# Two of four FFN block pairs issued one step sooner, with their tile's projections, in a hand-ordered recurrent and FFN kernel

## The reference, cut to what matters

```python
xn = layernorm(x)                                   # x: (2, 2048, 256)
s  = timemix(xn)                                    # RWKV-7 mixing, with a recurrence over time
g  = silu(ffn(xn))
return x + s * g

def timemix(x):
    dx  = x_last - x;  mix = tanh((x + dx*x_miu) @ x_A)
    miu = lambdas + einsum(mix, x_B)                # 6 mixes
    r_in, w_in, k_in, v_in, a_in, g_in = x + dx * miu
    v = v_in @ vW.T;  r = r_in @ rW.T;  g = tanh(g_in @ g_A) @ g_B
    w = -softplus(-(w_miu + tanh(w_in @ w_A) @ w_B)) - 0.5
    k = normalized(k_in @ kW.T + tanh(k_in @ k_A) @ k_B)
    a = sigmoid(a_time + a_in @ a_A @ a_B) * 2
    kk = k * exp(min(w*0.5, 0))
    # per head, S is 64x64:  S = S*exp(w) + (S@-k) (k*a)^T + v kk^T ;  y = S @ r
    y = wkv7(r, w, kk, v, -k, k*a)
    return (groupnorm(y) + bonus(r, k, v)) * g @ oW.T

def ffn(x):                                         # 8 experts, top 2, rank-16 corrections
    top2 = top_k(softmax(x @ gate_w.T + gate_b))
    for e in top2: out += gate_e * (relu(x@wi.T + bi + x@lora_A[e].T@lora_B[e].T) @ wo.T + bo)
```

## Time and profile before

| | |
|---|---|
| median of 3 runs | 1036.86 us (1034.81 to 1039.39) |
| the profiled execution | 1039.15 us |
| its span, first to last instruction | 1037.4 us |
| PE busy | 997.8 us, 96% |
| DVE busy | 839.3 us, 81% |
| ACT busy | 664.8 us, 64% |
| POOL busy | 457.1 us, 44% |
| granted TensorE clock, mean | 0.987 of full |
| chain that ended last, PE's share | 91% |

### The profile page before, as it was taken

One profiled execution on the slowest core, in us unless ns is written; L12 is line 12 of the kernel. 1 busy time (PEld: TensorE's weight loads), 2 busy tenths in 40 slices (PEclk: granted clock), 3 DMA queues, 4 the chain that ended last, 5 costly groups with the idle time before them and its releaser, 6 DMA issues.

```text
span 1037.4 us, 45407 instructions
## 1 busy us (share of the span) xinstructions
PE 997.8 (96%) x19910; PEld 781.1 (75%) x19910; DVE 839.3 (81%) x1674; ACT 664.8 (64%) x1461; POOL 457.1 (44%) x541
## 2 busy tenths in 40 slices
PE   5799999999999999999999999999999999999896
PEld 3487777778787787877777787777878778787674
DVE  4377888888888797988888898888889879798854
ACT  2457666676757667575766866577685666757553
POOL 2344262534536254453635436354443725445422
PEclk8799999999999999999999999999999999999997
DMA  7000000000000000000000000000000000000000
GB/s 245 1 13 3 2 3 23 3 4 22 4 22 4 22 3 3 22 5 22 3 23 3 3 23 3 22 4 3 23 3 23 3 23 3 3 22 4 12 4 22
DMA packets 9268, 17.13 MB, mean 17 GB/s; under 512 B 1905, under 2 KB 3825, under 8 KB 8817
## 3 DMA queue, kind: packets, MB, share of 16 engines
q1 hardware_dynamic: 9072, 14.23, 4.3%
HBM read 10.03 MB, written 4.19 MB: 14 GB/s over the span
## 4 chain that ended last, share of the span: by engine, by line
PE 91%; DVE 4%; issue 2%; ACT 2%; SPq 0%; DMA 0%; POOLq 0%; POOL 0%; DVEq 0%
PE bank L250 37%; PE bank L249 14%; PE grams L457 10%; PE bank L334 5%; PE grams L526 2%; PE bank L472 2%; PE bank L483 2%; PE bank L516 2%; PE grams L431 2%; PE bank L557 2%; PE grams L581 2%; PE bank L349 2%; PE grams L546 2%; PE bank L293 2%; PE bank L365 2%
## 5 line engine op out<-in xcount | busy, mean ns | idle before, releaser
L1192 POOL TENSOR_TENSOR bk<-bk,tot 128x256 f32<-128x256 f32 x192 | 154.5, 816 | 215.7 <-PE grams L457 215.7
L1504 DVE COPY_PREDICATED gm<-c_mask_g,grams 128x1024 f32<-128x1024 int32 x96 | 160.1, 1667 | 14.1 <-PE grams L457 14.1
L879 ACT ACTIVATE relu<-bank,prm 128x256 f32<-128x256 f32 x256 | 107.1, 470 | 87.2 <-PE bank L250 85.9
L1173 POOL TENSOR_TENSOR xd<-mtmp,xnc 128x512 f32<-128x512 f32 x96 | 120.7, 1271 | 41.0 <-DVE mtmp L1370 41.0
L250 PE MATMUL bank<-xnc,w_wi 128*128 128x256 f32 x512 | 124.6, 386 | 4.2 <-ACT scratch L1159 2.1
L457 PEld LDWEIGHTS grams<-ar,bk 64*64 64x64 f32 x6144 | 100.1, 134 | 23.4 <-issue 15.3
L981 ACT ACTIVATE gl<-gm 32x128 f32<-32x128 f32 x320 | 98.8, 309 | 28.6 <-DVE gm L1504 21.9
L250 PE MATMUL bank<-xmt,w_lora_B 128*128 128x256 f32 x444 | 114.8, 387 | 0.2 <-issue 0.2
L457 PE MATMUL grams<-ar,bk 64*64 64x64 f32 x6144 | 111.0, 220 | 2.8 <-ACT scratch L1159 2.3
L250 PEld LDWEIGHTS bank<-xnc,w_wi 128*128 128x128 f32 x512 | 94.3, 190 | 22.4 <-issue 7.3
L1514 DVE TENSOR_TENSOR ar<-ar,tot 128x512 f32<-128x512 f32 x96 | 93.0, 968 | 21.2 <-PE grams L457 21.0
(11 more groups left out here) (189 smaller groups left out, 2200.3 us busy)
## 6 DMA issues: line engine op xcount, KB each, us to landing
x_in<-x SPq DMA_DIRECT2D x16, 256.0 KB, 2.9
out<-out_t SPq DMA_DIRECT2D x16, 256.0 KB, 2.1
w_wi<-w_wi_dram SPq DMA_DIRECT2D x1, 1024.0 KB, 6.9
w_wo<-w_wo_dram SPq DMA_DIRECT2D x1, 1024.0 KB, 9.1
w_lora_B<-w_lora_B_dram SPq DMA_DIRECT2D x1, 512.0 KB, 8.5
w_x_A<-w_x_A_dram SPq DMA_DIRECT2D x1, 256.0 KB, 2.8
w_x_B<-w_x_B_dram SPq DMA_DIRECT2D x1, 256.0 KB, 2.9
w_kW<-w_kW_dram SPq DMA_DIRECT2D x1, 256.0 KB, 3.4
```

The source lines that it names most:

```text
L879: A(dst[:, p % 2, j * 256:(j + 1) * 256], ZB[p % 2][:, j * 256:(j + 1) * 256], ACT.Relu, bias=prm[:, P_BI + 2 * p + j:P_BI + 2 * p + j + 1 ...
L1173: tt(xd[:, q, :, :], mtmp[:, k % 2, :, :], xnc[steps["front"] % 2][:, :, :], ALU.add).then_inc(S(f"xd_{k}_done"), 1)
L1192: tt(v, v, d, ALU.mult).then_inc(S(f"bk{k}_scaled"), 1)
L1504: run(v.copy_predicated(dst, msk.to_broadcast([128, 32, HALF // m, m]), src), "g_stored")
```

## The change

The pairs 0 and 1 (`EARLY`) of a tile's FFN are issued one step sooner, in the step of the tile's front; the pairs 2 and 3 stay with the recurrence. A step in the middle has as many FFN blocks as before: two of the tile in front, two of the tile behind. Step 1 gets two pairs that it did not have, and step 17 keeps two of its four. `xmt_` moves from the end of the front to its middle, since the early pairs need it. The sum of the four `down` in the last bank now begins with `down(0)` at the end of one step and ends in the next.

```diff
+EARLY = (0, 1)
...
+        def of(p):
+            return steps["front" if p in EARLY else "rec"]
...
-        GROUPS = [FIRST, SECOND, [k for k in names if k not in FIRST + SECOND]]
+        THIRD = ["wi", "lora_B"]
+        GROUPS = [FIRST, SECOND, THIRD, [k for k in names if k not in FIRST + SECOND + THIRD]]
...
             def base(p, half=False):
-                pe.wait_ge(*till("xnc_done", 0))
+                t = of(p)
+                pe.wait_ge(*until("xnc_done", t, 1))
...
+            def warm(n):
+                for _ in range(n):
+                    mm(CB[:, 0:256], xnc[1][:, 0, 0:128], xnc[1][:, 1, :], start=True, stop=True)
...
                 if step == 1:
-                    mm(bank[6][:, 0:128], ident[:], ident[:], start=True, stop=True)
+                    warm(6)
...
                         miu(0)
+                        wait_loaded(pe, 2)
+                        base(1)
                         pe.wait_ge(*till("mx_0_done", 2))
                         pe.wait_ge(*till("mx_1_done", 2))
                         miu(1)
+                        base(0)
...
                     if rec:
-                        base(1)
-                        lora(1)
+                        base(3)
                         barrier(step)
                         gram(0)
-                        base(0)
-                        lora(0)
+                        base(2)
...
-            wait_loaded(pe, 0)
-            pe.wait_ge(zeroed, NZ)
+            pe.wait_ge(zeroed, len(xnc))
...
-            wait_loaded(act, 0)
             act.wait_ge(zeroed, NZ)
...
             dve.wait_ge(zeroed, NZ)
-            wait_loaded(dve, 0)
-            v.tensor_copy(first_rows, eye32[:].unsqueeze(1).to_broadcast([128, 8, 32]))
+            dve.wait_ge(x_first, 16)
```

More of the change, by code:

```diff
@@ L309, in xt_ @@
                 pe.wait_ge(*till("xn_done", G))
+                if not steps["front"]:
+                    wait_loaded(pe, 0)
                 to_channels(used_by("xt"), xn, "xt_mm")
@@ L663, in tile @@
                         inv_x(3)
-                        base(2)
+                        diff(2)
                         inv_off(3)
@@ L718, in tile @@
                     if rec:
+                        lora(3)
                         gram(1)
-                        diff(0)
                     if front:
@@ L724, in tile @@
                     if rec:
-                        base(3)
+                        diff(2)
+                        diff(3)
                         gram(2)
@@ L733, in tile @@
                     if rec:
-                        base(2)
-                        lora(3)
-                        lora(2)
                         inv_x(1)
+                        down(2)
                     if front:
@@ L741, in tile @@
                         miu(1)
-                    if rec:
-                        gram(3)
-                        inv_off(1)
-                    if front:
+                        base(0, half=True)
+                        base(1, half=True)
                         pe.wait_ge(*till("mx_3_done", 2))
@@ L796, in tile @@
                         y_state(0)
+                    if front:
+                        diff(0, half=True)
+                    if rec:
+                        rec_inc(0)
+                        rec_y(0)
                     if front:
@@ L887, in xnc_e @@
                 act.wait_ge(*till("xt_mm", 1))
+                if not steps["front"]:
+                    wait_loaded(act, 0)
                 A(xnc[steps["front"] % 2][:, :, :], used_by("xt")[:, :], ACT.Copy).then_inc(S("xnc_done"), 1)
@@ L1350, in dx_ @@
                 dve.wait_ge(*till("xnc_done", 1))
+                if not steps["front"]:
+                    wait_loaded(dve, 0)
                 run(v.tensor_tensor(dc[:, :, 0, :, 0], xp[:, :, 1, :, STEPS - 1], xc[:, :, 0, :, 0], ALU.subtract), "dx_done")
@@ L1673, in tile @@
                         dx_()
+                    if rec:
+                        scale_ar(0)
+                    if front:
                         xm_()
+                        first_expert()
                     if rec:
```

606 lines of the change are left out of this document (308 added, 298 removed).

## The result

The changed kernel is slower by 1.5%: 1053.85 us, the median of 4 runs (1050.94 to 1055.71), against 1038.03 (1034.81 to 1039.39, 4 runs on the same chip). The ratio is 1.0151, 95% interval 1.0125 to 1.0177. The forecast was 1031.9 with a range up to 1038.0, and the time lies outside it.

A forecast was written before the change was run, and what follows sets the result against it. PE's stream of products was taken to bound the 14 full steps, some 860 of 1037 us. Terms -7.0 - 2.5 + 3.2 + 1.3 = -5.0 us from 1036.86 gave 1031.9 us, range 1026.5 to 1038.

The forecast's parts named there:

- Full steps: Steps 3 to 16: same work, only the number of array shape changes can differ; +1.3 us, bounds -2 and +6.
- Shapes: Full steps: each change of array shape costs 0.095 us, 40 changes a step instead of 39, over 14 steps.
- The rival on VectorE: Full steps: VectorE comes late to `gram(1)`, stalling 0.3 us in each of 14 steps, 4.2 us: 1036.1 us; chance 0.14.
- The slower rival: Full steps: VectorE's tail holds `gram(0)`, 0.9 us excess paid 14 times, +12.6 us: 1044.5 us; chance 0.08.
- Step 1: First step: early loads lost waiting for `lora_B`, `base(1)` delays `miu(1)`, added FFN work; +3.2 us, bounds -2 and +7.
- Step 17: Two FFN pairs leave this step, partly on its path; -7.0 us, bounds -10.8 and -2.
- The second part: Step 17 from `rec_p(0)` to VectorE's end mark: PE loses 6.9 us of work, 2.9 and 0.8 us counted as saved.
- The levels: Step 17 from `gram(0)` to `rec_p(0)`: first level stays 4.45 us, five later ones take 3.8; 3.3 us less.
- Barriers: Barriers of steps 3 and 17: PE work beside ACT's long copy cuts waits from 4.4 to 1.9 us; -2.5, bounds -4.4 and 0.

The follow-up runs named there:

- Experiment 1: Changed kernel with five small VectorE operations a step, the search for the second expert, left out: 1041.59 us, ratio 1.0033 to the kernel before.
- run 9: Changed kernel with the second expert's search ahead of `mixed(1)`, `base(0)` ahead of `miu(1)`, and POOL's `bv_` behind the last `scale_bk(5)`: 1047.15 us, ratio 1.0093.
- 2: Changed kernel with the second expert's search moved ahead of `mixed(1)` and `base(0)` ahead of `miu(1)`: 1052.44 us, ratio 1.0135.
- 3: Changed kernel with POOL's `bv_` moved from ahead of `mixed(2)` to between `mixed(3)` and `mixed(5)`: 1048.32 us, ratio 1.0100.
- 5: Changed kernel with POOL's `bv_` moved from ahead of `mixed(2)` to behind the last `scale_bk(5)`: 1050.10 us, ratio 1.0119.
- experiment 7: Changed kernel with `bv_` behind the last `scale_bk(5)`, plus five product groups issued as halves, five more shape changes a full step: 1060.41 us, ratio 1.0217.
- experiment 11: Kernel before with only the new loading: four load groups, later waits for the first, six warming products: 1034.25 us, ratio 0.9971.
- run 10: As run 9, plus step 1 with key norm ahead of `r_` and `base(0)` behind `miu(2)`, and step 17 with `bv_` behind the last `scale_bk`: 1047.01 us.
- experiment 8: Changed kernel with `bv_` behind the last `scale_bk(5)`, plus three groups halved: 20 more PE instructions, no more shape changes: 1049.76 us, ratio 1.0116.
- runs 5 to 8: Four changed kernels with `bv_` behind the last `scale_bk(5)`: alone, with step 1 reordered (1045.38 us), and with two sets of halved groups: 1045.38 to 1060.41 us.

## Why the prediction was wrong

**Full steps, the step that failed.** "The full steps. The FFN and projection work is the same. What can change is how often the array's shape changes" gave +1.3 us, bounds -2 and +6. It measured +17.9: 14.1 from the longer clean step and 3.8 from issue stalls. (With the barrier's -1.6 this is the +16.3 above.) The prediction's sum had no term for PE waiting on VectorE inside the step. I compared what PE does and not when its data come. The steps before were busy for 61.26 of 61.30 us, and I took that for a property of the work; it was one of the order. In the new order VectorE has the search and the masks ahead of `mixed(4)`, in the part of the step in which POOL is busy. Experiment 1 shows that VectorE's lateness there is the cause: 0.88 of 1.01 us go with five operations, which is 12.3 of the 14.1 us. That POOL's exclusion makes it late rests on the rows that end together and on the two kinds of steps in run 9. No run took the exclusion away: moving work around (2, 3, 5, 9) shifted it to the next operation and gave back at most 0.57.

**Shapes.** The term itself was sound. The price was 0.095 by the earlier trace rows and 0.11 by experiment 7. What is left in a clean step without the wait is 0.13 us, one or so change a step as counted.

**The rival on VectorE** had the mechanism but the place wrong. I followed VectorE for the first 8 us of the step, up to `gram(1)`, and found 7.9 to 8.4 against 8.1. `gram(1)` was not late. The wait came 27 us into the step. I had applied the exclusion of POOL to `store(0)`, where a row of before showed it, and priced the small operations at the 0.2 us that they took beside an idle POOL. The trace of before had the other price too. Its `lg`, 16 numbers a partition, ends at 256.60, when a pair of POOL's products ends at 256.57:

```profile
254.08 2.49 POOL L1173 TENSOR_TENSOR xd<-mtmp,xnc 128x512 f32<-128x512 f32 x2
255.81 0.79 DVE L1376 TENSOR_TENSOR lg<-rt,w_gate_b 128x16 f32<-128x16 f32 x1
```

The slower rival (VectorE's tail holds `gram(0)`) did not occur: PE waited for VectorE's mark only in steps 2 and 17, 0.35 and 0.61 us, and in step 18, where it had waited before. What it was built on, one excess paid in each step, did.

**Step 1**: +3.2 forecast, +3.9 measured by one profile of each kernel. With the spread of 3.3 us between profiles of one order, the agreement to 0.7 us is partly luck. `miu(1)` ended at 24.48 (forecast 24.5), `base(1)` took 3.8 us at the lower clock (3.5), and the transfer was waited for until 18.98 (19.3):

```profile
18.98 3.78 PE L258 MATMUL bank<-xnc,w_wi 128*128 128x256 f32 x8 [4.05 <-DMA w_lora_B<-w_lora_B_dram]
```

The sum hid two large terms: by these profiles the loads gain 4.9 us in this step (experiment 11, mark at 46.14 against 51.07), and the FFN blocks cost 8.9. The sizes are rough. Experiment 11's profile was the fastest of its 12 runs, and by the medians its whole gain is 3.2 us.

**Step 17**: -7.0 forecast, -5.4 from `gram(0)` to the end mark (49.0 to 43.6). The second part, from `rec_p(0)` on, came as forecast: 18.6 us, 3.7 less. The levels shortened by 1.7 us instead of 3.3, and the first alone took 5.30 instead of 4.45, since POOL's `bv_` now held `gram(1)` for 1.35 us:

```profile
1003.65 1.17 PE L473 MATMUL grams<-ar,bk 64*64 64x64 f32 x64 [1.35 <-POOL bk L1210]
```

In run 10, with `bv_` behind the last `scale_bk`, the first level took 4.29 us.

**Barriers**: -2.5 forecast. PE's waits fell from 4.4 to 0.62 and 0.61 us, -3.2. In time, mark to mark, it is -1.6 at step 3 and -0.3 at step 17. With these the parts are 3.9 + 1.1 + 17.9 - 1.9 - 5.4 - 0.1 = 15.5 us.

**Open.** The "issue" stalls add 3.8 us over steps 3 to 16 (step lengths over the clean one, less the barrier: 2.4 us before, 6.2 after, 5.6 in experiment 1, so the wait is not their cause). They stand at `inv_x` and `inv_off`, but neither the number of instructions (experiment 8) nor a wait explains them. Step 2's 1.1 us I have not taken apart. It has the same wait as the full steps, and took 62.26 instead of 63.24 us in experiment 1. But runs 5 to 8 have it at 62.1 to 62.7 with the wait in place. No order was tried that keeps VectorE's masks clear of POOL altogether.

## What to carry to other kernels

When an order is changed, walk the whole step on the engine next in load and not only to its first meeting with the bound engine. VectorE was busy for only 84% of the step, and still had no slack where its work is dense. Take lengths from start to start and look at the rows of the weight loads too: the busy share of PE, and its own waits, hid most of this one. Price small VectorE operations by what POOL does beside them, since each can take as long as a whole POOL instruction. Test the parts of a combined change apart: here the loading alone was a gain and the order hid it.

## What the runs showed of the hardware

- A VectorE operation on 16 numbers a partition took 0.17 us alone and 0.87 to 1.27 us beside POOL, and ended with POOL's instruction.
- Whether the two collide can differ from step to step in one kernel: in run 9 the same operation took 1.27 us in five full steps and 0.17 in nine.
- PE started a group 0.05 us after the last VectorE result that it needed. Such a wait was printed at the weight loads (0.36 us) where it was not printed at the products, and `kW` then took 1.92 instead of 1.82 us.
- A change of array shape cost 0.11 us, and 20 more instructions in a step cost nothing.
- With the order of step 1 unchanged, the granted clock was full again from 22 us in one profile and from 28 in another, and step 1 took 53.8 to 57.1 us.
